# Latent attention: row sums written with the exps, in place of products with ones

## The reference

```python
q = (x @ Wqa @ Wqb).reshape(b, s, H, D)
kv = (x @ Wkva @ Wkvb).reshape(b, s, KVH, D, 2)
...
k = jnp.repeat(k, g, axis=2)
v = jnp.repeat(v, g, axis=2)
scores = jnp.einsum('bqhd,bkhd->bhqk', q, k) * scale
scores = jnp.where(causal[None, None], -jnp.inf, scores)
w = jax.nn.softmax(scores, axis=-1)
out = jnp.einsum('bhqk,bkhd->bqhd', w, v).reshape(b, s, E)
return out @ Wout + bout
```

## Time and profile before

| | |
|---|---|
| median of three runs | 2121.06 us |
| profiled execution, its own time | 2123.64 us |
| its span, first to last instruction | 2121.8 us |
| TensorE, ScalarE, VectorE, GpSimd busy in the span | 94%, 80%, 72%, 69% |
| latent attention stage | about 1784 to 2018 us |
| granted TensorE clock, mean of the span | 0.98 |

### The profile page before, as it was taken

One profiled execution on the slowest core, in us unless ns is written; L12 is line 12 of the kernel. 1 busy time (PEld: TensorE's weight loads), 2 busy tenths in 40 slices (PEclk: granted clock), 3 DMA queues, 4 the chain that ended last, 5 costly groups with the idle time before them and its releaser, 6 DMA issues. The chain is left out here.

```text
span 2121.8 us, 64825 instructions
## 1 busy us (share of the span) xinstructions
PE 1998.5 (94%) x21611; PEld 1398.7 (66%) x21611; DVE 1536.9 (72%) x3516; ACT 1692.7 (80%) x4279; POOL 1455.7 (69%) x1662
## 2 busy tenths in 40 slices
PE   6799999999999999999999999999999998988696
PEld 3566666666666666666666666666666765655486
DVE  7777777777777777777777777777777764788654
ACT  3688888888888888888888888889898985655355
POOL 5777777777777777777777777777777762344343
PEclk9899999999999999999999999999999998999888
DMA  4222232322232222332223232223534242000023
GB/s 110 50 63 64 47 94 58 73 47 63 64 84 62 64 47 64 80 73 59 61 50 91 63 70 51 59 68 80 129 83 97 56 100 84 2 12 12 14 61 107
DMA packets 191396, 138.95 MB, mean 65 GB/s; under 512 B 47758, under 2 KB 183636, under 8 KB 191172
## 3 DMA queue, kind: packets, MB, share of 16 engines
q1 hardware_dynamic: 189028, 133.09, 26.4%
q0 software_dynamic: 2272, 4.72, 0.7%
HBM read 28.36 MB, written 14.96 MB: 20 GB/s over the span
## 5 line engine op out<-in xcount | busy, mean ns | idle before, releaser
L976 ACT ACTIVATE pr<-bank,mx 128x64 f32<-128x64 f32 x1536 | 336.8, 348 | 0.3 <-DVE mx L1079 0.2
L1161 POOL TENSOR_TENSOR qr<-t 128x512 f32<-128x512 f32 x192 | 245.9, 1281 | 119.5 <-DVE t L1059 119.4
L1058 DVE TENSOR_TENSOR t<-bank,rot_t 128x512 f32<-128x512 f32 x384 | 263.0, 685 | 87.9 <-PE bank L813 85.3
L1149 POOL TENSOR_TENSOR qr<-qr,rn 128x512 f32<-128x512 f32 x192 | 200.6, 1045 | 173.3 <-DVE rn L1030 173.3
L1059 DVE TENSOR_TENSOR t<-bank,rot_t 128x512 f32<-128x512 f32 x384 | 261.5, 681 | 0.0
L1164 POOL TENSOR_TENSOR kr<-t 128x512 f32<-128x512 f32 x192 | 245.9, 1281 | 0.1
L1167 POOL TENSOR_TENSOR sqh<-sq 128x512 f32<-128x512 f32 x192 | 245.8, 1280 | 0.0
L938 ACT ACTIVATE sq<-bank 128x512 f32<-128x512 f32 x192 | 114.3, 596 | 158.2 <-DVE t L1059 158.0
L984 ACT ACTIVATE kBD<-bank 64x512 f32<-64x512 f32 x384 | 229.0, 596 | 3.1 <-PE bank L531 0.8
L813 PE MATMUL bank<-wqkv,xs 128*128 128x512 f32 x384 | 207.2, 622 | 10.1 <-issue 3.5
L864 PE MATMUL bank<-kBD,qT 128*32 128x128 f32 x6144 | 207.5, 276 | 0.4 <-ACT bank L918 0.3
(11 more groups left out here) (256 smaller groups left out, 4337.1 us busy)
## 6 DMA issues: line engine op xcount, KB each, us to landing
vBD<-vS SPq DMA_DIRECT2D x1152, 64.0 KB, 2.0
vBD<-vS SPq DMA_DIRECT2D x576, 32.0 KB, 1.8
wqkv<-in_L_ffn_Wqkv_dram SPq DMA_DIRECT2D x12, 768.0 KB, 6.5
rows<-const SPq DMA_DIRECT2D x4, 2244.0 KB, 11.0
wo<-in_L_ffn_Wo_dram SPq DMA_DIRECT2D x12, 256.0 KB, 2.9
t<-rows SPq DMA_DIRECT2D x39, 66.0 KB, 1.8
vBD<-in_L_ffn_W_dram SPq DMA_DIRECT2D x1, 2048.0 KB, 8.6
vBD<-in_L_ffn_W_dram SPq DMA_DIRECT2D x8, 256.0 KB, 7.0
```

Of the source, the lines that this page charges most:

```text
L976: ins = act.activation(pr[:, slot % 2, hd, :], bank[5][:, hd * 64:(hd + 1) * 64], ACT.Exp, bias=mx[:, slot % 2, hd:hd + 1])
L1058: dve.tensor_tensor(t1[:, m], src, tab[:, 0, :].unsqueeze(1).broadcast_to([P, HH, DH]), ALU.mult)
L1149: pool.tensor_tensor(x, x, rn[:, slot, half * HH:(half + 1) * HH].unsqueeze(2).broadcast_to([P, HH, DH]), ALU.mult).then_inc(norm.sem, 1)
L1161: pool.tensor_tensor(qr[:, slot].rearrange("p (h d) -> p h d", d=DH), t1[:, 0], t2[:, 0], ALU.add).then_inc(q_add.sem, 1)
```

## The change

ScalarE gives each exp a second output, its row sum, into `csum`. VectorE takes the reciprocal of the 128x32 sums of a sequence; GpSimd spreads each over the 8 columns of its head (`cinx`, in the space of `wo`); TensorE turns the two tiles into the second half of bank 2 in quad 0 of the next step; ScalarE copies them to `crd`, behind its exps of r0, and the `xnG` copy now stands behind that too. VectorE's product waits for `c_keep`. TensorE's first turns of quad 0 wait for it as well. The products with ones, `conesb`, its set-up on GpSimd and the wide reciprocal go.

```diff
--- before.py
+++ after.py
@@ -177,8 +177,9 @@
         cqa, ckva = sb("cqa", [QL, SEQ]), sb("ckva", [KVL, SEQ])
         ck = sb("ck", [P, SEQ])
         cvn = sb("cvn", [P, NT, KVH, QD])
-        conesb = sb("conesb", [P, GRP, 32])
         cnb = sb("cnb", [P, KVH, GRP])
+        csum, cinv = sb("csum", [P, NT, KVH, GRP]), sb("cinv", [P, NT * QH])
+        cinx = wo[:, :, :].rearrange("p c d -> p (c d)")[:, 0:SEQ]
 
         late = kBD[:, :, :, :, :].rearrange("p h q e k -> p (h q e k)")
         ckm = late[:, 0:2048].rearrange("p (j k) -> p j k", j=2 * GRP)
@@ -316,9 +317,9 @@
         c_ckm = sig("c_ckm", per=2)
         c_s, c_max, c_exp, c_pt = (sig(x, credit=12) for x in ("c_s", "c_max", "c_exp", "c_pt"))
         c_pta, c_ptd = sig("c_pta", credit=6), sig("c_ptd", credit=6)
-        c_vz, c_one = sig("c_vz"), sig("c_one")
-        c_o = sig("c_o")
-        c_nrm = sig("c_nrm", per=2, credit=2)
+        c_vz = sig("c_vz")
+        c_o, c_back, c_keep = (sig(x) for x in ("c_o", "c_back", "c_keep"))
+        c_nrm = sig("c_nrm", per=3, credit=2)
         c_y, c_res = sig("c_y"), sig("c_res", credit=3)
 
         LN_STEPS, LOGIT, ROWS, ROW_SET, ROWS_END, DIFF, MEMBER, PLACE, GATE_STEPS = 3, 1, 1, 9, 12, 14, 18, 20, 20
@@ -1439,6 +1440,8 @@
                 for r in range(KVH):
                     G = NG * a + KVH * m + r
                     pe.wait_ge(c_exp.sem, c_exp.after(G))
+                    if a and (m, r) == (0, 0):
+                        pe.wait_ge(c_keep.sem, c_keep.after(a - 1))
                     if g is not None and (m, r) == (0, 0):
                         pe.wait_ge(g_out.sem, g_out.after(g))
                     if g is not None and g >= 1 and (m, r) == (0, 1):
@@ -1461,16 +1464,14 @@
                     pe.wait_ge(c_nrm.sem, c_nrm.after(a - 1))
                 for x in range(4):
                     j, kb = j0 + x // nk, x % nk
-                    for o, ones in ((0, False), (SEQ, True)):
-                        for r in range(KVH):
-                            mm = pe.matmul(bank[1][32 * r:32 * r + 32, o + t * P:o + (t + 1) * P],
-                                           conesb[:, j, :] if ones else cvj[:, kb, r, j, :], cpT[r][:, x * P:(x + 1) * P],
-                                           start=(m == 0 and x == 0 and not ones), stop=(x == 3), skip_group_check=True)
+                    for r in range(KVH):
+                        mm = pe.matmul(bank[1][32 * r:32 * r + 32, t * P:(t + 1) * P], cvj[:, kb, r, j, :],
+                                       cpT[r][:, x * P:(x + 1) * P], start=(m == 0 and x == 0), stop=(x == 3),
+                                       skip_group_check=True)
                 mm.then_inc(c_o.sem, 1)
 
             pe.wait_ge(cast_done.sem, 2)
             pe.wait_ge(f_res.sem, f_res.after(NI - 1))
-            pe.wait_ge(c_one.sem, 2)
             pe.wait_ge(ld_late.sem, 16 * (BLANKS + 1))
             for s, par, live in pairs():
                 a, c = s - 1, s - 2
@@ -1493,9 +1494,16 @@
                             for t in range(NT):
                                 mm = pe.transpose(low[:, t * P:(t + 1) * P], xcols(s * NT + t), ident)
                             mm.then_inc(ln_t1.sem, 1)
+                        if live(2):
+                            pe.wait_ge(c_pta.sem, c_pta.after(2 * (NQ * c + 2) + 1))
+                            pe.wait_ge(c_nrm.sem, c_nrm.after(c, 2))
+                            for t in range(NT):
+                                mm = pe.transpose(bank[2][:, SEQ + t * P:SEQ + (t + 1) * P],
+                                                  cinx[:, t * P:(t + 1) * P], ident)
+                            mm.then_inc(c_back.sem, 1)
                         if live(3):
-                            n = NQ * c + 2 if live(2) else NQ * NB - 1
-                            pe.wait_ge(c_pta.sem, c_pta.after(2 * n + 1))
+                            if not live(2):
+                                pe.wait_ge(c_pta.sem, c_pta.after(2 * (NQ * NB - 1) + 1))
                             choose_turn(pe, s - 3, 1 - par)
                         if live(2):
                             values(c, 2)
@@ -1550,10 +1558,6 @@
                 a = s - 1
                 for m in range(NQ):
                     t, j0, nh, nk = QUADS[m]
-                    if m == 0 and live(3):
-                        act.wait_ge(g_back.sem, g_back.after(s - 3))
-                        act.wait_ge(d_lmm.sem, d_lmm.after(s - 4))
-                        act.activation(xnG, bank[2][:, 0:SEQ], ACT.Copy).then_inc(g_out.sem, 1)
                     if m == 2 and live(0):
                         act.wait_ge(lat_mm.sem, lat_mm.after(s))
                         act.wait_ge(c_pq.sem, c_pq.after(s - 1))
@@ -1573,9 +1577,18 @@
                             act.wait_ge(c_pt.sem, c_pt.after(G - KVH))
                             n = nk * P
                             for hh in range(nh):
-                                ins = act.activation(cp[:, r, hh * n:(hh + 1) * n], bank[4 + r][:, hh * n:(hh + 1) * n],
-                                                     ACT.Exp, bias=cnb[:, r, hh:hh + 1])
+                                ins = act.activation(cp[:, r, hh * n:(hh + 1) * n], bank[4 + r][:, hh * n:(hh + 1) * n], ACT.Exp,
+                                                     bias=cnb[:, r, hh:hh + 1], accum_out=csum[:, t, r, j0 + hh:j0 + hh + 1])
                             ins.then_inc(c_exp.sem, 1)
+                        if r == 0 and m == 0 and live(2):
+                            act.wait_ge(c_back.sem, c_back.after(s - 2))
+                            if live(3):
+                                act.wait_ge(g_back.sem, g_back.after(s - 3))
+                            act.activation(crd, bank[2][:, SEQ:2 * SEQ], ACT.Copy).then_inc(c_keep.sem, 1)
+                        if r == 0 and m == 0 and live(3):
+                            act.wait_ge(g_back.sem, g_back.after(s - 3))
+                            act.wait_ge(d_lmm.sem, d_lmm.after(s - 4))
+                            act.activation(xnG, bank[2][:, 0:SEQ], ACT.Copy).then_inc(g_out.sem, 1)
                         if r == 0 and m == 0 and live(0):
                             ln_keep(act, LN_C + s, bank[0][:, 0:SEQ], acc[:, seq_cols(s)])
                         if r == 0 and m == 1 and live(0):
@@ -1622,8 +1635,7 @@
                             ln_moments(dve, LN_C + s, tokens(s))
                         if live(2):
                             dve.wait_ge(c_o.sem, c_o.after(NQ * c + 2))
-                            dve.reciprocal(crd, bank[1][:, SEQ:2 * SEQ]).then_inc(c_nrm.sem, 1)
-                            dve.wait_ge(c_nrm.sem, c_nrm.after(c, 1))
+                            dve.wait_ge(c_keep.sem, c_keep.after(c))
                             dve.tensor_tensor(con, bank[1][:, 0:SEQ], crd, ALU.mult).then_inc(c_nrm.sem, 1)
                     if m == 1 and live(3):
                         choose_bias(dve, s - 3)
@@ -1654,6 +1666,9 @@
                                 add_stream(dve, s + 1)
                     elif m == 0 and live(-1):
                         add_stream(dve, s + 1)
+                    if m == 2 and live(1):
+                        dve.wait_ge(c_exp.sem, c_exp.after(NG * a + NG - 1))
+                        dve.reciprocal(cinv[:, :], csum[:, :, :, :].rearrange("p t r j -> p (t r j)")).then_inc(c_nrm.sem, 1)
                     if m == 1 and live(2):
                         gate_moments(dve, c)
                     if m == 2 and live(2):
@@ -1664,11 +1679,6 @@
             prepare(pool, 0, 0)
             pool.tensor_copy(causal[:, :, :], cst("causal").rearrange("p (t q) -> p t q", t=NT)).then_inc(cast_done.sem, 1)
             pool.tensor_copy(identb[:, :], ident).then_inc(cast_done.sem, 1)
-            pool.memset(conesb[:, :, :], 0.0).then_inc(c_one.sem, 1)
-            pool.wait_ge(c_one.sem, 1)
-            for j in range(GRP):
-                ins = pool.memset(conesb[:, j, j * QD:(j + 1) * QD], 1.0)
-            ins.then_inc(c_one.sem, 1)
             pool.wait_ge(add_u.sem, 1)
             pool.wait_ge(ld_late.sem, 16 * (BLANKS + 1))
             pool.memset(cvj, 0.0).then_inc(c_vz.sem, 1)
@@ -1695,6 +1705,11 @@
                     gate_rsqrt(pool, s - 2)
                 if live(0):
                     prepare(pool, s, par)
+                if live(1):
+                    pool.wait_ge(c_nrm.sem, c_nrm.after(s - 1, 1))
+                    if s > 1:
+                        pool.wait_ge(c_back.sem, c_back.after(s - 2))
+                    pool.tensor_copy(cinx.rearrange("p (h d) -> p h d", d=QD), cinv[:, :].unsqueeze(2).broadcast_to([P, NT * QH, QD])).then_inc(c_nrm.sem, 1)
                 if live(2):
                     twin_rows(pool, s - 2, par, live(4))
 
```

## The result

The changed kernel takes 2147.31 us (median of four runs, 2145.85 to 2148.45) against 2121.43 beside it: +25.9 us, a ratio of 1.0118 with a 95% interval of 1.0106 to 1.0131. The forecast was slower, +10.3 us. The direction is right, the time lies in the range, and the size is too small by a factor of 2.5. The profiled execution spans 2145.4 us, 23.6 more than before.

What follows compares the result with a forecast made beforehand. A ring of waits through TensorE, VectorE and ScalarE, no engine full, bounds the attention stage. Early and steady steps add 12.1 us, the tail takes 1.8: +10.3, or 2131.4 us against 2121.06; range 2116 to 2156.

Steps and rivals of the forecast that it cites:

- Price of a sum: ScalarE's queue time for each exp's row-sum output, 256 exps in all: taken as 0.10 us, bounded by 0 and 0.31.
- Quads 1 and 2 hide eight sums each: In a steady step, +0.8 us of exps in each of these quads is covered by other waits: 0.
- Quad 0 pays 1.0 us: In a steady step's quad 0, longer exps delay the last turns from 1894.57 to 1895.5: +1.0 us.
- Products with ones are worth nothing in the ring: Removing them saves TensorE 2.6 us a step, but waits for copies, the rope product and ScalarE absorb nearly all.
- the ring: A step's chain of waits through TensorE, VectorE and ScalarE: scores, maxima, exps, turns, copies, next scores; 27.09 us when steady.
- Nearly all 2.6 us turns into idle time of TensorE: Per step, the time freed by removing products with ones becomes TensorE waiting in all three quads.
- The return chain hides: Reciprocal, spread, transposes and copy of the sums finish before TensorE needs them in quad 0, with 1.1 us to spare.
- Tail -1.8: After the steady steps, less reciprocal and value-block time outweighs the last quads' dearer exps: -1.8 us.
- First quad 0 +1.6: The stage's first quad 0, without xnG copy or routing, pays for its exps' sums: +1.6 us.
- rival D: TensorE's clock falls to its lower level for a third of each step: +30 us on top, about 2160; chance 0.06.
- the new quad 0 should be like the former: Quad 0's clock should hold as in a window at 0.98 with 3.77 of 6 us busy.
- One sign named ahead: The forecast is wrong if the stage's clock row reads under 1.0 from step 2 on.

Runs made afterwards that it cites:

- e8: Changed kernel with sums from the exps in quads 1 and 2 only, quad 0 keeping its products with ones: 2122.00 us, 1.0001 of the kernel before.
- e1: Changed kernel with the products with ones put back, their output unread: 2138.35 us, 1.0079 of the kernel before.
- e5: Changed kernel with products with ones put back, plus unread identity products filling TensorE's waits ahead of the turns: 2132.14 us, 1.0044 of the kernel before.
- e10: Changed kernel, without products with ones, plus unread identity products filling TensorE's waits ahead of the turns: 2134.06 us, 1.0041 of the kernel before.
- e4: Kernel before with only its products with ones removed, the reciprocal taken of the value half: 2129.51 us, 1.0028 of the kernel before.
- e2: Changed kernel without the exps' sums, csum set once to ones: 2124.48 us, 1.0008 of the kernel before.
- e3: Kernel before with the sums added to its exps, unread, products with ones and reciprocal kept: 2148.48 us, 1.0110 of the kernel before.

## Why the forecast was right, and where it failed

- *Price of a sum*: taken 0.10 us, measured 0.085 (256 columns) and 0.094 (128). The row it was taken from, a small operation squeezed between others, was the right neighbour; the lone one of 0.203 us less the overlap gives the same. The Trainium skill says of VectorE that an operation which also writes out its accumulator is two instructions ("VectorE: DVE Perf Modes", "Two Vector instructions with no wait between them"). ScalarE did likewise here: a second record for each of 256 exps. The Trainium skill's other rule, the sum added as each result passes ("ScalarE activation tables: per-element evaluation and per-set limits", "What a function is on this engine"), may hold for the adding; it says nothing of the read, which is the record that the trace adds.
- *Quads 1 and 2 hide eight sums each*: right (18.04 us against 18.05; e8).
- *Quad 0 pays 1.0 us*: 0.83 at a clock of 1.00 (e1, e5, e10). The seven steps take 9.5 us more in e10, for 10.5.
- *Products with ones are worth nothing in the ring*: right in the ring (27.05 us, e4). But "Nearly all 2.6 us turns into idle time of TensorE" put the price of that idle time at nothing.
- *The return chain hides*: right. GpSimd's spread took 0.40 us at 1896.43, TensorE's transposes started at 1897.87 without waiting.
- *Tail -1.8*: e10 shows 39.12 us for 40.71, -1.6. *First quad 0 +1.6*: not seen; before ran that quad at the lower clock (four scores 1.69 us at 1791.84), e10 at the higher.
- **The step that failed is the clock, kept out of the sum as rival D** at a chance of 0.06, because "the new quad 0 should be like the former" window, which held 0.98 with 3.77 of 6 us busy. One window had been made a rule: the changed kernel's 6 us from 1902 to 1908 were busy for 4.48 and read 0.60. Its mechanism came true beside the forecast's, in all seven steps (0.84 to 0.93). I had priced it at +30 for a third of each step and left it out of the sum; the runs show 13 us (e10): 10 in the steps, 2.5 in the tail, 1.4 behind the stage, less 0.5 ahead of the steps. The two were treated as cases that exclude each other, and they are terms of one sum: the sums lengthen ScalarE's path and with it TensorE's waits, and with the waits filled the clock stays up (e10). One sign named ahead did show it, the clock row under 1.0 in the stage. Another came out the other way for the same reason: TensorE's busy time in the seven steps, forecast to shrink, is 164.6 us for 161.4, since at the lower clock its products last longer.
- *Luck*: e10's span is 10.1 us longer than before's, as if the 10.3 were met. The ring and the tail gave 7.8 of it; 2.3 came behind the stage, where the forecast had nothing, and the +1.6 of the first quad 0 did not come.

What stays open is which wait brings it down. In the profiled executions the longest single wait of TensorE in a steady step was 0.42 us in e5, 0.78 in e10, 0.96 in before and 1.08 in e8, whose steady steps all stood at 1.00. It was 1.12 in e2 and e4, with a fall in two of four steady steps and in one of four. In the changed kernel, e1 and e3 each quad 0 waited about 1.32 us (the changed kernel also 1.67 in quad 1 where the clock was up), and all, four and all of their seven steps read under 1.00. But length alone does not fix it. TensorE's timeline of e1, of e8 and of before:

```profile
1957.83 0.63 PE L1455 MATMUL bank<-const,qr 128*128 128x128 f32 x4 [1.32 <-ACT vS L1571]
1959.72 1.14 PE L1432 MATMUL bank<-kBD 32*128 32x512 f32 x8
...
1823.26 1.07 PE L1455 MATMUL bank<-const,qr 128*128 128x128 f32 x8 [1.48 <-ACT vS L1569]
...
1789.86 2.06 PE L1451 MATMUL bank<-const,qr 128*128 128x128 f32 x8 [0.96 <-ACT vS L1565]
```

In e1 the work behind 1.32 us of waiting, and in e8 that behind 1.48 us, ran at full speed; in before's first quad 0 that behind 0.96 us did not. So the waits make falls likely and do not fix them; their length and their sum were not varied apart.

## What to carry to other kernels

When work is taken from an engine that another one paces, look for what the idle time does, not only for what it does not give: TensorE's idle stretches can cost more than the work did (e4), and a few products that nobody reads, placed in the waits, can give it back (e5, e10). A small output added to many short operations costs time on the engine's queue by its own record, 0.09 us each here, and was free only in those quads where another engine came last. Put two mechanisms that feed each other into one sum, not into two rivals.

## What the runs showed that was not expected

- ScalarE's read of the sum lasts 0.19 to 0.34 us in its record and takes 0.085 to 0.094 us of the queue.
- TensorE's clock fell with the busy share of a step as high as in before: e3 does all of before's products and fell, e8 does 1.6 us less in a step than before (21.91 for 23.50 us busy) and held 1.00 in all steady steps.
- Falls cost 1.2 to 2.3 us a step (each of the changed kernel's seven against e10's), 1.5 to 1.6 in the steady steps of e2 and e4. The one looked at outlasts the wait by some 10 us (1903 to 1914 in the changed kernel) and meets the scores and a value block.
- An execution without a trace can differ from the profiled one: six of e4's eight runs took 4 to 6 us more than the one that was profiled, at a lower mean clock.
